# SyncE's order of a turn, the order of attention's steps, and norms that add a negated mean, in a fused attention and mixture-of-experts layer

## The reference

```python
x = x + attention(layernorm(x), W_Q, W_K, W_V, W_O)   # 16 heads of 16, causal, softmax
x = x + moe(layernorm(x), gate_w, w_gate_up, w_down, shared weights)
# layernorm: (x - m) / sqrt(v + 1e-5), without weights
# moe: 16 experts, the 2 best of each token, renormalised; plus a shared expert of width 704
```

## Time and profile before

| | |
|---|---|
| median of 3 runs | 848.94 us (847.85 to 850.78) |
| the profiled execution, its own time | 845.39 us |
| its span, first to last instruction | 843.7 us |
| mean granted TensorE clock | 0.932 |
| attention half, until the first transpose of the second half on TensorE | 487.8 us |
| busy over the span | TensorE 87%, VectorE 62%, ScalarE 48%, GpSimd 43% |

### The profile page before, as it was taken

The page is one execution under the profiler, slowest core; times in us unless marked ns, Lnnn a source line. Parts: engine busy times, 40 slices in busy tenths (PEclk is TensorE's granted clock), DMA queues, the critical chain, the costliest instruction groups (busy, mean ns, idle before and its releaser), DMA issues. The chain is left out here.

```text
span 843.7 us, 17080 instructions
## 1 busy us (share of the span) xinstructions
PE 735.6 (87%) x5970; PEld 579.9 (69%) x5971; DVE 524.6 (62%) x1158; ACT 401.8 (48%) x777; POOL 359.5 (43%) x664
## 2 busy tenths in 40 slices
PE   2479698997999989999987587989699999999997
PEld 1356475575666767657563467878689999988886
DVE  6276586785877858778770358555635444556667
ACT  3116554564565655656565222433446555642222
POOL 4303537264292652926366203757600000067771
PEclk9779898998999989999997778999989999999999
DMA  5657468284583856828232222977755465368763
GB/s 150 235 214 265 138 249 277 77 281 170 199 284 121 280 172 221 281 84 322 73 99 73 88 75 79 308 246 242 237 179 155 158 193 174 123 199 256 252 217 128
DMA packets 102503, 159.72 MB, mean 189 GB/s; under 512 B 7712, under 2 KB 78368, under 8 KB 98208
## 3 DMA queue, kind: packets, MB, share of 16 engines
q1 hardware_dynamic: 96288, 141.99, 50.1%
q0 software_dynamic: 6144, 16.79, 5.9%
HBM read 86.66 MB, written 71.83 MB: 188 GB/s over the span
## 5 line engine op out<-in xcount | busy, mean ns | idle before, releaser
L607 DVE TENSOR_REDUCE neg_max<-ps_w 128x1 f32<-128x512 f32 (+3 forms) x352 | 201.9, 634 | 57.1 <-PE ps_w L712 57.0
L544 ACT ACTIVATE probs<-ps_w 128x512 f32<-128x512 f32 x320 | 165.4, 625 | 41.1 <-PE ps_w L728 41.1
L395 POOL TENSOR_TENSOR pool_scratch<-minus_half 1x1 f32<-1x1 f32 x190 | 34.8, 183 | 252.5 <-ACT probs L544 213.4
L1095 POOL DMA_INDIRECT ex<-yg_dram,slots x64 | 65.0, 1016 | 154.4 <-DMA yg_dram<-y 135.2
L425 POOL TENSOR_SCALAR_AFFINE_SELECT probs<-probs 128x256 f32<-128x256 f32 (+1 forms) x224 | 93.8, 430 | 0.0
L1083 POOL DMA_INDIRECT xg_dram<-srow,slots x64 | 66.0, 1032 | 52.3 <-DVE slots L1246 27.9
L739 PE MATMUL ps_w<-probs,v_aug 128*32 128x512 f32 (+3 forms) x1024 | 79.7, 455 | 3.7 <-POOL probs L425 3.7
L177 PE MATMUL ps_f<-stacks 128*128 128x512 f32 x176 | 73.3, 416 | 10.3 <-DVE xT_lo_f L1264 6.8
L1112 ACT ACTIVATE silu<-ps_f 128x512 f32<-128x512 f32 (+1 forms) x48 | 28.5, 594 | 105.8 <-PE ps_f L179 105.8
L178 PE MATMUL ps_f<-xT_lo_f,stacks 128*128 128x512 f32 x176 | 71.6, 407 | 0.0
L179 PE MATMUL ps_f<-stacks 128*128 128x512 f32 x176 | 71.5, 406 | 0.0
(11 more groups left out here) (169 smaller groups left out, 1842.6 us busy)
## 6 DMA issues: line engine op xcount, KB each, us to landing
qk_dram<-projected SPq DMA_DIRECT2D x96, 256.0 KB, 3.4
stacks<-qk_dram SPq DMA_DIRECT2D x16, 1024.0 KB, 6.0
xg_dram<-zeros SPq DMA_DIRECT2D x20, 512.0 KB, 10.8
srow<-xg_dram SPq DMA_DIRECT2D x40, 256.0 KB, 2.8
q_st<-qk_dram SPq DMA_DIRECT2D x8, 1024.0 KB, 4.9
k_st<-qk_dram SPq DMA_DIRECT2D x8, 1024.0 KB, 8.3
projected<-experts SPq DMA_DIRECT2D x16, 384.0 KB, 4.5
yg_dram<-projected SPq DMA_DIRECT2D x20, 256.0 KB, 2.2
```

The costliest lines, as they stand in the source:

```text
L544: act.activation(probs[:, g, p * PAIR + half * BANK:p * PAIR + (half + 1) * BANK], ps_w[:, plan.bank(kind, which, half), :], ACT.Exp).then ...
L607: dve.tensor_reduce(out=neg_max[u][:, qt, first:first + len(heads)], in_=bank[:, 0:len(heads) * width].rearrange("p (h n) -> p h n", h=len ...
L1095: pool.indirect_dma_start(out=back[:, m, c, :], out_offset=None, in_=yg_rows, in_offset=bass.IndirectOffsetOnAxis(ap=slots[:, c, m:m + 1], ...
```

## The change

Three edits in `build_attention`. First, SyncE's order in `body`. Two DMAs of zeros follow the load of xb, and the third stands between the first stacks' way out and back; the rows of maxima of unit 0 stand ahead of the stacks of unit 0, and those of unit 1, with the store of xn2, ahead of the way back of unit 1's stacks; the store of x1 is last. In the last turns the loads of shared weights move with them. Second, `TURN` begins five steps later, so that xT, the pair S(·,1,0,2) and S(·,1,0,3) and oT stand at its end, one batch later; some steps change places: xT ahead of S(·,1,0,3), the maxima 4 of the next batch behind both, one pair of maxima (1, 0, 1) between mT(0, 1) and S(0, 1, 0, 0), S(0, 0, 0, 3) ahead of O(-1, 1), S(0, 0, 0, 4) behind half of V, x2T ahead of S(0, 0, 1, 4), and W. Third, `layer_norm` makes a negated mean and adds it instead of subtracting the mean.

```diff
 TURN = [
-    ("S", -1, 1, 0, 2), ("max", 0, 0, 4), ("S", -1, 1, 0, 3), ("oT", -1, 1), ("xT", 1, 0), ("xT", 1, 1), ("Q", 1, 1), ("S", -1, 1, 0, 4),
-    ("S", -1, 1, 1, 0), ("max", 0, 0, 5), ("Q", 1, 0), ("S", -1, 1, 1, 1), ("max", 0, 0, 6), ("R", -2), ("S", -1, 1, 1, 2), ("K", 1, 0),
-    ("S", -1, 1, 1, 3), ("S", -1, 1, 1, 4), ("max", 0, 0, 7), ("PV", -1, 2), ("max", 0, 0, 8), ("max", 0, 0, 9), ("max", 0, 0, 10),
-    ("max", 0, 1, 0), ("PV", -1, 3), ("oT", -1, 2), ("mT", 0, 0), ("oT", -1, 3), ("max", 0, 1, 1), ("max", 0, 1, 2), ("oTT", -1, 0),
-    ("oTT", -1, 1), ("K", 1, 1), ("max", 0, 1, 3), ("S", 0, 0, 0, 0), ("max", 0, 1, 4), ("O", -1, 0), ("S", 0, 0, 0, 1), ("S", 0, 0, 0, 2),
-    ("O", -1, 1), ("S", 0, 0, 0, 3), ("W", 8, 4), ("S", 0, 0, 0, 4), ("S", 0, 0, 1, 0), ("moments_x1", -1), ("V", 1, 0), ("max", 0, 1, 5),
-    ("S", 0, 0, 1, 1), ("W", 7, 0), ("V", 1, 1), ("max", 0, 1, 6), ("max", 0, 1, 7), ("max", 0, 1, 8), ("PV", 0, 0), ("S", 0, 0, 1, 2),
-    ("max", 0, 1, 9), ("S", 0, 0, 1, 3), ("max", 0, 1, 10), ("W", 7, 1), ("moments_x", 2), ("S", 0, 0, 1, 4), ("x2T", -1, 0),
-    ("x2T", -1, 1), ("max", 1, 0, 0), ("max", 1, 0, 1), ("mT", 0, 1), ("oT", 0, 0), ("W", 7, 2), ("W", 7, 3), ("L", -1, 0), ("W", 8, 5),
-    ("PV", 0, 1), ("max", 1, 0, 2), ("S", 0, 1, 0, 0), ("S", 0, 1, 0, 1), ("L", -1, 1), ("max", 1, 0, 3),
+    ("max", 0, 0, 4), ("Q", 1, 1), ("S", -1, 1, 0, 4), ("S", -1, 1, 1, 0), ("max", 0, 0, 5), ("Q", 1, 0), ("S", -1, 1, 1, 1),
+    ("max", 0, 0, 6), ("R", -2), ("S", -1, 1, 1, 2), ("K", 1, 0), ("S", -1, 1, 1, 3), ("max", 0, 0, 7), ("S", -1, 1, 1, 4), ("PV", -1, 2),
+    ("max", 0, 0, 8), ("max", 0, 0, 9), ("max", 0, 0, 10), ("max", 0, 1, 0), ("PV", -1, 3), ("oT", -1, 2), ("mT", 0, 0), ("oT", -1, 3),
+    ("max", 0, 1, 1), ("max", 0, 1, 2), ("oTT", -1, 0), ("oTT", -1, 1), ("K", 1, 1), ("max", 0, 1, 3), ("S", 0, 0, 0, 0),
+    ("S", 0, 0, 0, 1), ("W", 8, 4), ("O", -1, 0), ("max", 0, 1, 4), ("W", 7, 0), ("W", 7, 1), ("S", 0, 0, 0, 2), ("S", 0, 0, 0, 3),
+    ("O", -1, 1), ("moments_x1", -1), ("V", 1, 0), ("S", 0, 0, 0, 4), ("S", 0, 0, 1, 0), ("max", 0, 1, 5), ("V", 1, 1), ("max", 0, 1, 6),
+    ("S", 0, 0, 1, 1), ("max", 0, 1, 7), ("max", 0, 1, 8), ("PV", 0, 0), ("S", 0, 0, 1, 2), ("max", 0, 1, 9), ("S", 0, 0, 1, 3),
+    ("max", 0, 1, 10), ("x2T", -1, 0), ("x2T", -1, 1), ("S", 0, 0, 1, 4), ("moments_x", 2), ("max", 1, 0, 0), ("mT", 0, 1), ("oT", 0, 0),
+    ("W", 7, 2), ("L", -1, 0), ("W", 7, 3), ("max", 1, 0, 1), ("PV", 0, 1), ("max", 1, 0, 2), ("S", 0, 1, 0, 0), ("S", 0, 1, 0, 1),
+    ("L", -1, 1), ("max", 1, 0, 3), ("W", 8, 5), ("S", 0, 1, 0, 2), ("oT", 0, 1), ("xT", 2, 0), ("xT", 2, 1), ("S", 0, 1, 0, 3),
 ]
...
+    minus_mean = [sb(f"minus_mean{n}", [P, TB], f32) for n in range(2)]
...
         def zero_rows(n):
+            if n >= ZERO_DMAS:
+                return
...
                 sp.dma_start(xb[:, :, :], x_v[it + 2]).then_inc(x_in, 16)
+            zero_rows(3 * it)
+            zero_rows(3 * it + 1)
             if before:
...
                 sp.dma_start(x1[:, :, :], x_v[it - 1]).then_inc(xres_in, 16)
-            if after:
-                stack_out_of_sbuf(it + 1, 0)
-            if this:
-                max_rows(it, 0)
             if it == B - 1:
                 shared_weights(0)
                 shared_weights(1)
                 sp.wait_ge(xn2_out, 16)
                 sp.dma_start(xn_f, xn2_v[0]).then_inc(first_in, 16)
+            if this:
+                max_rows(it, 0)
+            if after:
+                stack_out_of_sbuf(it + 1, 0)
+            zero_rows(3 * it + 2)
+            if it == B:
+                shared_weights(4)
+                shared_weights(5)
             if after:
                 stack_back(it + 1, 0)
+            if it == B - 1:
+                shared_weights(2)
+                shared_weights(3)
+            if after:
                 stack_out_of_sbuf(it + 1, 1)
+            if this:
+                max_rows(it, 1)
+            if before:
+                sp.wait_ge(xn2_done, it)
+                sp.dma_start(xn2_v[it - 1], xn2[:, :, :]).then_inc(xn2_out, 16)
+            if after:
                 stack_back(it + 1, 1)
             if before:
                 sp.wait_ge(freed["dve"], plan.freed("O", (it - 1, 1))[1])
                 sp.dma_start(x1_v[it - 1], x1[:, :, :]).then_inc(x1_out, 16)
-            for n in range(it * 3, min(it * 3 + 3, ZERO_DMAS)):
-                zero_rows(n)
-            if it == B - 1:
-                shared_weights(2)
-                shared_weights(3)
-            if this:
-                max_rows(it, 1)
-            if it == B:
-                shared_weights(4)
-                shared_weights(5)
-            if before:
-                sp.wait_ge(xn2_done, it)
-                sp.dma_start(xn2_v[it - 1], xn2[:, :, :]).then_inc(xn2_out, 16)
...
+            if apply:
+                chain.step(pool.tensor_scalar(out=minus_mean[n][:, :], in0=mv[:, :, 0], scalar1=-1.0, scalar2=None, op0=ALU.mult))
...
-                out = pool.tensor_scalar(out=target[:, t, :], in0=source[:, t, :], scalar1=mv[:, t, 0:1],
-                                         scalar2=rstd[n][:, t:t + 1], op0=ALU.subtract, op1=ALU.mult)
+                out = pool.tensor_scalar(out=target[:, t, :], in0=source[:, t, :], scalar1=minus_mean[n][:, t:t + 1],
+                                         scalar2=rstd[n][:, t:t + 1], op0=ALU.add, op1=ALU.mult)
```

## The result

The changed kernel takes 803.99 us (median of four runs, 800.10 to 805.15), the one before 848.39 beside it (847.53 to 850.78): ratio 0.9464, 95% interval 0.9427 to 0.9502. That is 44 us faster where 30.5 were forecast. The profiled execution took 800.1, so against the 845.4 of the one before there are 45.3 us to find.

What follows compares the result with a forecast made beforehand. TensorE sets the pace, held up by waits for rows of maxima, xT and masks, and by slow clock. Terms 13.8 + 11 + 3.5 + 2.2 = 30.5 us took the profiled 845.4 to 814.9, median 818; range 806 to 840.

Steps and rivals of the forecast that it cites:

- The clock: TensorE's half-clock stretches after S(it,1,0,0) waits: of up to 17.0 us lost, two thirds come back, −11 us.
- The wait for the rows: TensorE's wait before S(it,1,0,0) for the DMA of rows of maxima: 16.7 us falls to about 2.9, −13.8 us.
- Rival 2: Rows of maxima stay late, from DMA itself or the stores around, not the zeros: about 840 us; chance 0.12.
- Q: TensorE's wait before Q(·,1) for VectorE's lower xT: 1.6 falls to 1.0 in six turns, −3.5 us with fewer waits.
- Turn 7: Last attention turn, TensorE's wait before PV(7,1) for GpSimd's masks: 2.2 of 3.7 us go, −2.2 us.
- The norm: GpSimd's layer norm in attention: add and multiply takes 605 ns instead of 1212, so x2T and xT do not stall.
- Rival 1: In GpSimd's norms add costs what subtract costs, so x2T and xT stall and two slow stretches come: 834 us; chance 0.24.
- Rival 3: First stacks return late on SyncE's queue, delaying the next batch's maxima: 844 to 856 us; chance of a slower end 0.05.
- The signs: Measurements in TensorE's waits, clock, turn times and GpSimd's add and multiply that would show the forecast right.
- The 46.7: Turn 5 before the change, 50.2 us at full clock, less its S and Q waits: a turn without waits, 46.7 us.

Runs made afterwards that it cites:

- S alone: Only SyncE's order changed against the kernel before, steps and norms as before: 821.98 us, ratio 0.9720.
- S with N: SyncE's order and the norms changed against the kernel before, old order of steps kept: 819.11 us, ratio 0.9665.
- S with T: SyncE's order and the order of steps changed against the kernel before, norms still subtracting: 815.16 us, ratio 0.9640.
- the kernel with the two more steps: Changed kernel with S(-1,1,0,4) ahead of Q(1,1) and GpSimd's lower half of shared weights 4 ahead of x1's last norm: 802.30 us.

## Why the prediction fell short, point by point

The direction, the mechanism and most signs of it were right. The size was not: 803.99 lies below the range's lower end of 806. On the profiled executions 45.3 us came where the sum has 30.5.

**The clock: the step that failed.** It reads "I leave about half the turns a stretch of 3.4 or one longer, 6 us in cost: −11 us". None stayed: all six stretches are gone, worth 15.1 us by the time in which TensorE was busy in them (half of 30.2) and 17.0 at most. The reason given was turn 6, with a slow stretch beside a wait of only 0.6 us. That row is right, but nothing like it came back: from 61.6 us to the end of turn 6 the changed kernel, with no wait above 1.0, has no stretch at all, and with waits of 3.0 put back there is one in seven turns of seven. In between it goes both ways: turns 3 and 4 of the kernel before had a stretch behind S waits of 1.3 and 2.0, turn 5 none behind 1.7; S alone has three stretches of 3.4 behind Q waits of 1.6 to 1.8, S with N has the same Q waits and none. What decides there, and why turn 6 of the kernel before had its stretch, stays open. The first and the last of S alone's three stretches:

```profile
90.90:94.30 3.40, 3.40 (x12) 2.36 (x14) 0.00 (x0) 0.57 (x1) 0.00 (x0) 0.50 1.09 384
...
336.70:340.10 3.40, 3.40 (x17) 2.04 (x16) 1.73 (x3) 2.66 (x5) 0.76 (x2) 0.50 1.09 385
```

Caution of a third on this term was too much once the forecast took its cause, the long waits, as gone.

**The wait for the rows.** The forecast took turn 6's 5.2 us from mT to S as the price and left 0.2 to 0.3 in each turn, 1.1 in turn 0: −13.8. It was −16.7. Turn 6 still had two zeros, the ways back and the x1 store ahead of the rows, and its row names VectorE's maxima as what came last; on a clear queue the rows need 4.0 to 4.1, which any cover of 5 us hides, even the old list's 4.6 (S alone waits for none). The price was read from a row in which what was to be removed was still partly there. Rival 2, that the rows stay late, is out: with the zeros moved and the other two edits, 13.3 of the 16.7 are gone, and the rest of the order takes the last 3.4.

**Q.** 0.7 remained in a full turn where 1.0 was forecast, 4.3 in all: −5.2 instead of −3.5.

**Turn 7.** PV(7,1) gave 1.9 of the 2.2, but a later PV waits 2.0 for masks in its place, so nothing is gained there on balance. The 3.1 us that turn 7 and the end of attention took less come beside it: the slow stretches there add up to 13.9 us instead of 24.8, and 0.9 of waiting for xn is gone, while x2T(7) waits 1.6 longer for VectorE. That 2.2 were forecast and 3.1 came is luck.

**The norm.** The forecast went by the rows, took 605 ns and a stall of nothing; it was 547, and nobody waits. Rival 1's way of working out what the norm would cost otherwise, 1.0 for x2T and 0.5 for xT a turn, was near: S with T, which is that case but for the negation, waits 1.1 a turn and 7.8 in turns 0 to 6, and is 11 us slower than the whole change where 16 were said. The two slow stretches that the rival added did not come. The GPSIMD Engine Reference of the Trainium skill (§ 3.1, Elementwise side-by-side cycle accounting) prices a body of up to two operations alike; 543 and 1220 ns for the same tile differ from that, and the measurement decides.

**Rival 3.** The first stacks came 0.3 us late, once, in turn 0: the margin of −0.9 to 1.1 us that was worked out for it was real, and the price of no importance.

**The signs.** Rows of maxima under 5 us in all: none in turns 0 to 6, 0.3 in turn 7 as before. Clock of full turns 0.98 or more: 1.00. Turns of 48 to 49 us: 47.0, lower by the clock term and the waits above. Q about 1.0: 0.7. Add under 700 ns: 547. The 46.7 worked out for a turn without waits was right: 47.0 less Q's 0.7 is 46.3.

**The sum.** On the profiled executions 14.8 us more came than the sum has. Turns 0 to 6 are 36.7 us shorter where the terms for them (rows, clock, Q) have 28.3: 8.4 of the 14.8. The rows gave 16.7, Q 5.2 and the clock 15.1, and the short waits for VectorE, ScalarE and one DMA grew from 2.2 to 3.1, which makes 36.1; 0.6 stay open. So the clock was 4.1 short, the rows 2.9 and Q 1.7. Another 0.9 lie in turn 7, and 3.9 ahead of turn 0 and 1.5 in the second half, where nothing was forecast. The 3.9 at the start come with a slow stretch of 10.2 us in place of one of 20.5. Seven of the nine kernels with the new list of steps have 10.2 there and the other two 17.1; the four without it have 13.7 to 20.5. How the list does that, no run tells.

## What to carry to other kernels

A small transfer that an engine waits for can come late behind large ones on its queue, as the rows of maxima did: put it ahead of bulk traffic that nobody waits for, and read its price from a place where the queue is clear, or say that none is. A wait that repeats in every turn can cost twice, once as idle time and once as work at half the clock behind it; where the waits went here, the second part went with them, but for three stretches in S alone. Edits that shift slack between engines must be judged together: the cheaper norm was worth nothing alone and 11 us once SyncE's order and the order of steps had come to lean on it.

## What the runs showed that was not expected

A subtract on GpSimd makes a two-operation instruction on 128x256 cost 1220 ns instead of 543, in either place of the pairs run here; negating one 128x4 tile first (236 ns) saves 2.7 us (4 x 665 ns) in four tiles.

VectorE's last norm got slower by the change, though no line of it was touched. VectorE's timeline in the changed kernel, and GpSimd's beside it:

```profile
433.20 2.86 DVE L580 TENSOR_SCALAR xn<-x,mean_var,rstd 128x256 f32<-128x256 f32 x4 [1.75 <-POOL rstd L411]
...
433.15 1.79 POOL L488 TENSOR_TENSOR w_lo<-projected,stacks 128x768 fp32r<-128x768 f32 x1
```

Before, these four tiles took 1.38 us with nothing of GpSimd beside them. In the kernel with the two more steps GpSimd's subtract is done at 424.57, and the four take 1.38 again:

```profile
430.24 1.38 DVE L581 TENSOR_SCALAR xn<-x,mean_var,rstd 128x256 f32<-128x256 f32 x4 [1.74 <-POOL rstd L411]
...
422.72 1.85 POOL L488 TENSOR_TENSOR w_lo<-projected,stacks 128x768 fp32r<-128x768 f32 x1 [7.33 <-ACT stacks L565]
```

So this instruction of GpSimd beside it, which reads two tiles, cost VectorE 1.48 us here, and TensorE's wait for x2T(7) was longer by about as much, 7.2 against 5.8.
